# Attention output in row-tiled products, and its projection in the same two PSUM banks

## The chip, the cores and the metric

The kernel runs on one core of a Trainium2 chip. The metric is the time of the whole program on the device, in microseconds (us). Engines: PE multiplies matrices into PSUM (eight banks of 512 f32 columns on 128 partitions), DVE, ACT and POOL do the other arithmetic, SP issues most DMAs. Each engine runs its own instructions in order, and semaphores tie them.

## The reference, cut to what matters

128 samples of 64 tokens with 128 features. A layer normalisation and a cross-attention with 16 heads of 8 features stand first, then three feed-forward blocks of two linear layers each (weights dequantised, with low-rank parts), whose middle has a layer normalisation and a GELU.

```python
q = heads(layernorm(x) @ Wq.T + bq); k = heads(ctx @ Wk.T + bk); v = heads(ctx @ Wv.T + bv)
score = einsum('bhij,bhkj->bhik', k, q) / sqrt(8)
attn  = softmax(score, axis=1)                       # over the heads
out   = einsum('bhik,bhij->bhjk', attn, v)           # sum over the keys i
x     = x + (out as tokens x 128) @ Wo.T + bo
x     = x + ffn(layernorm(x))                        # three blocks
```

The softmax runs over the heads, not over the keys.

## The kernel before

The tokens are cut into 16 chunks of 512 (four tiles of 128 tokens, eight samples). A chunk has four pairs of samples. On its 128 partitions a pair has the keys of its two samples, 64 each; for every head there are 64 queries. Every engine walks the chunks c = 0 to 17 in four steps p = 0 to 3 (`chunk(c, par, half)`); chunks 2 to 11 are a hardware loop over two chunks, the rest is written out. Step n = 4c + p works on several pairs at once:

- PE: the scores of pair n + 1 into `score_ps` (L1439); the shift of pair n by its maxima (L1591, behind DVE); something for chunk c + 2 (context transposes, query, key or value projection); a part of the output projection of an earlier chunk (`project_out`, L1427); probabilities times values of pair n - 2 into `att_ps` (L1648, behind POOL and, for a chunk's first pair, behind ACT); remainders or input transposes for chunk c + 2.
- DVE: maxima over the heads for pair n (L840); in step 1 the input statistics of chunk c + 3 (L624); for pair n - 1 the sum over the heads (L856) and its reciprocal (L859); in step 3 the residual addition for chunk c - 2, out of `wo_ps` (L863).
- ACT: the exponentials of pair n (L1164), and most evacuations, among them `att_ps` to `att_t` in step 2 (L1203) and the value blocks (L1083) in step 3.
- POOL: probabilities times the reciprocal for pair n - 1 (L527), and the small variance work of inputs and layers.

**Probabilities times values.** The values lie in `v_diag`: for each pair and head a block of 32 columns. The rows are the pair's 128 keys. Of the 32 columns a head fills 8 for sample 0 and 8 for sample 1 (on the other sample's rows these are zero), and the other 16 belong to its neighbour head. A product takes 128 rows, 32 columns of weights and 64 queries; four go to four column places of the array (`tile_position=(0, 32 * grp)`), and 16 products do a pair. The result holds eight heads by two samples on 128 partitions, once for each half `o` of the heads: the columns of `att_ps` are 256 for each half.

**Output projection.** Since a sample's features lie in two column halves, mixed with the other sample's, the weight `wo_t` exists four times (`[P, 2, 2, P]`: half, sample), with zeros in between. A tile of tokens takes two f32 products into `wo_ps`, behind a row product of 512 columns that opens the bank and puts the bias there. `bias_rows` and `project_out(0)` stand in step 3, tiles 1, 2 and 3 in the steps 0 to 2 of the next chunk, and the third raises `s_wo`. The bank may be opened when DVE has added the chunk before (`s_x2`).

**The turn.** Some feed-forward steps for the first chunks are put among the last chunks by a table (`EARLY`), and a third and a fourth one are written out by hand. `third_step_closes` on PE, at the end of (15, 3), is a second layer (L1694) behind ACT's first GELU; `third_step` on DVE stands in (16, 0) and takes in its result (L898). After chunk 17 the feed-forward steps run in a loop of their own.

Lines of the change: L660 and L712 to L720 (DVE: weight copies), L863 (addition), L1005 to L1017 (ACT: seeds, layers), L1083 (value blocks), L1151, L1203, L1353 to L1362 (PE: weight transposes), L1391, L1423, L1611 to L1654.

## Time and profile before

| | us |
|---|---|
| median of three runs | 358.87 (358.61 to 361.41) |
| the profiled execution, whole | 358.84 |
| its span, first to last instruction | 356.9 |
| PE busy | 340.4 |
| DVE busy | 327.8 |
| ACT busy | 289.0 |
| POOL busy | 267.3 |

The span is what the profiler sees of the program; about 2 us of the time lie around it. A row of the timeline gives the start, the length from the first start to the last end, engine, line, what is written from what, and how many records were merged. An f32 product that isn't a transpose has two records, each with a load of weights beside it (PEld). Records of one engine overlap at their ends, so what one thing costs is read from start to start.

### The profile page before, as it was taken

The numbers are of one execution on the slowest core, as the hardware profiler recorded it, in microseconds if no ns is written. First come the engines' busy times: TensorE is split into PE (matmuls) and PEld (weight loads), VectorE is DVE, ScalarE is ACT, GpSimd is POOL, SyncE is SP. The second block draws the span as 40 slices with busy tenths as digits, with TensorE's granted clock in tenths as the row PEclk, the third lists the DMA queues.
The fourth block names the chain that finished last, engine by engine and source line by source line (L and its number), as shares of the span: only waits on it lengthen the run. The fifth ranks groups of instructions, "written<-read, shape, count | busy, mean of one in ns | idle before, by whom it ended". The sixth has DMA issues, their size and how long they took to land.

```text
span 356.9 us, 13104 instructions
## 1 busy us (share of the span) xinstructions
PE 340.4 (95%) x4808; PEld 254.6 (71%) x4808; DVE 327.8 (92%) x822; ACT 289.0 (81%) x588; POOL 267.3 (75%) x288
## 2 busy tenths in 40 slices
PE   7979999999999999999999989978999999999995
PEld 6546567667767766766766767856888888888874
DVE  7889999999999999999999999878999999988774
ACT  4688888888878878887887868488989999999982
POOL 6448888877987987897799998878777778774231
PEclk9999999999999999999999999999999999999999
DMA  7978557648646744854753400000110001110112
GB/s 204 239 243 266 172 163 217 209 129 245 195 132 202 222 157 150 264 167 140 222 162 109 151 2 2 2 1 3 30 32 29 29 29 41 50 32 29 42 48 89
DMA packets 54530, 43.29 MB, mean 121 GB/s; under 512 B 4624, under 2 KB 48608, under 8 KB 54496
## 3 DMA queue, kind: packets, MB, share of 16 engines
q1 hardware_dynamic: 53920, 42.31, 39.4%
q10 hardware_dynamic: 576, 0.53, 0.5%
q8 instruction: 21, 0.34, 0.4%
q14 instruction: 13, 0.11, 0.1%
HBM read 26.05 MB, written 16.78 MB: 120 GB/s over the span
## 4 chain that ended last, share of the span: by engine, by line
PE 61%; DVE 23%; issue 6%; ACT 5%; POOL 4%; DMA 1%; DVEq 0%; ACTq 0%; POOLq 0%
PE score_ps L1687 8%; DVE zsum L856 6%; PE att_ps L1648 6%; PE score_ps L1591 6%; DVE negmax L840 5%; PE wo_ps L1427 5%; PE score_ps L1439 4%; PE score_ps L1781 3%; PE work L1463 3%; PE work L1774 3%; DVE st L886 3%; PE att_ps L1781 2%; PE work L1476 2%; PE work L1469 2%; PE score_ps L1681 2%
## 5 line engine op out<-in xcount | busy, mean ns | idle before, releaser
L527 POOL TENSOR_TENSOR probs<-probs,rz 128x1024 f32<-128x1024 f32 x64 | 136.3, 2141 | 27.3 <-DVE rz L859 27.3
L578 POOL TENSOR_TENSOR rs<-ve,minus_half 128x4 f32<-128x4 f32 (+1 forms) x47 | 55.7, 1186 | 34.7 <-DVE ve L786 24.1
L856 DVE TENSOR_REDUCE zsum<-probs 128x64 f32<-128x1024 f32 x64 | 77.3, 1208 | 2.4 <-ACT probs L1164 2.3
L1164 ACT ACTIVATE probs<-score_ps 128x1024 f32<-128x1024 f32 x64 | 65.6, 1025 | 14.5 <-PE score_ps L1591 13.9
L840 DVE TENSOR_REDUCE negmax<-score_ps 128x64 bf16<-128x1024 f32 x64 | 75.2, 1176 | 0.8 <-PE score_ps L1439 0.8
L1427 PEld LDWEIGHTS wo_ps<-wo_t,att_t 128*128 128x128 f32 x256 | 36.9, 191 | 13.4 <-issue 12.0
L1687 PEld LDWEIGHTS score_ps<-lin_t,h 128*128 128x128 f32 x304 | 36.9, 191 | 11.3 <-DVE h L939 7.1
L1648 PE MATMUL att_ps<-probs,v_diag 128*32 128x64 f32 x2048 | 43.4, 224 | 1.1 <-POOL probs L527 0.7
L1252 ACT ACTIVATE z<-score_ps,rs 128x128 f32<-128x128 f32 x152 | 43.6, 383 | 0.6 <-POOL rs L578 0.6
L1687 PE MATMUL score_ps<-lin_t,h 128*128 128x128 f32 x304 | 39.7, 278 | 1.9 <-DVE h L939 1.9
L1648 PEld LDWEIGHTS att_ps<-probs,v_diag 128*32 128x32 f32 x2048 | 32.8, 109 | 10.9 <-POOL probs L527 2.7
L1591 PE MATMUL score_ps<-negmax,ident_bf 128*128 128x512 bf16 x128 | 38.7, 384 | 0.6 <-DVE negmax L840 0.5
L1427 PE MATMUL wo_ps<-wo_t,att_t 128*128 128x128 f32 x256 | 38.1, 275 | 0.0
L859 DVE RECIPROCAL rz<-zsum 128x64 f32<-128x64 f32 x64 | 35.4, 553 | 2.2
L886 DVE BATCH_NORM_STATS2 st<-score_ps 128x6 f32<-128x128 f32 x152 | 33.7, 284 | 3.5 <-PE score_ps L1687 2.5
L1439 PE MATMUL score_ps<-q_stack,k_stack 64*64 64x128 f16 x1024 | 26.5, 222 | 1.9 <-DMA k_stack<-k_parts 0.8
L1439 PEld LDWEIGHTS score_ps<-q_stack,k_stack 64*64 64x64 f16 x1024 | 16.6, 106 | 13.4 <-issue 11.0
L476 POOL TENSOR_TENSOR half_rstd<-veps,minus_half 128x4 f32<-128x4 f32 x16 | 16.5, 1029 | 5.7 <-DVE veps L636 2.4
L1031 ACT ACTIVATE xln<-x_all,half_rstd 128x128 f32 (+1 forms) x60 | 19.0, 391 | 0.9 <-POOL half_rstd L476 0.9
L1263 ACT ACTIVATE g<-score_ps,cols 128x512 f32<-128x512 f32 x21 | 16.8, 800 | 2.8 <-PE score_ps L1681 2.8
L1774 PEld LDWEIGHTS work<-lin_t,g 128*128 128x128 f32 x104 | 13.7, 192 | 6.2 <-issue 6.2
L1083 ACT ACTIVATE v_diag<-work 64x512 f32<-64x512 f32 x30 | 17.6, 586 | 0.3
(278 smaller groups left out, 692.7 us busy)
## 6 DMA issues: line engine op xcount, KB each, us to landing
q_parts<-parts SPq DMA_DIRECT2D x15, 512.0 KB, 3.5
k_stack<-k_parts SPq DMA_DIRECT2D x30, 256.0 KB, 3.3
q_stack<-q_parts SPq DMA_DIRECT2D x60, 128.0 KB, 2.9
x_all<-in_x SPq DMA_DIRECT2D x16, 256.0 KB, 3.9
ctx_sb<-in_ctx SPq DMA_DIRECT2D x16, 256.0 KB, 3.7
k_parts<-parts SPq DMA_DIRECT2D x16, 256.0 KB, 2.9
out<-x_all SPq DMA_DIRECT2D x15, 256.0 KB, 2.3
q_parts<-parts SPq DMA_DIRECT2D x4, 128.0 KB, 2.3
```

Of the source, the lines that this page charges most:

```text
L527: nc.gpsimd.tensor_tensor(e[:, :, :, :], e[:, :, :, :], by_query.broadcast_to([P, BANDS, SEQ, ADJ]), ALU.mult).then_inc(s_probs, 1)
L578: nc.gpsimd.tensor_tensor(rs2[v][:, lo:hi], ve2[v][:, lo:hi], minus_half[:, lo:hi], ALU.pow).then_inc(p_rs[v], 1)
L840: nc.vector.tensor_reduce(negmax[p % 2][:, :], score_ps[p % 2][:, :].rearrange("p (h k) -> p k h", k=SEQ), AX_X, ALU.max, negate=True).the ...
L856: nc.vector.tensor_reduce(zsum[q][:, :], probs[(p - 1) % 4][:, :, :, :].rearrange("p u k s -> p k u s"), AX_XY, ALU.add).then_inc(s_zsum, 1)
L886: ins = nc.vector.bn_stats(st2[v][:, lo + i, :], src[:, TILE * i:TILE * (i + 1)])
L1164: nc.scalar.activation(probs[p][:, :, :, :], score_ps[p % 2][:, :].rearrange("p (u s k) -> p u k s", s=ADJ, k=SEQ), ACT.Exp, scale=SCALE). ...
L1252: ins = nc.scalar.activation(z[v][0][:, t, :], src[:, TILE * t:TILE * (t + 1)], ACT.Copy, scale=rs2[v][:, lo + t:lo + t + 1])
L1427: ins = nc.tensor.matmul(wo_ps[:, TILE * t:TILE * (t + 1)], att[:, o, TILE * u:TILE * (u + 1)], wo_t[:, o, b, :], start=False, stop=o == 1 ...
L1439: ins = nc.tensor.matmul(score_ps[mp % 2][SEQ * b:SEQ * (b + 1), c0:c0 + 2 * SEQ], k_stack[mb][half_rows, grp, k0:k0 + SEQ], q_stack[mb][h ...
L1591: ins = nc.tensor.matmul(score_ps[p % 2][:, CHUNK * o:CHUNK * (o + 1)], ident_bf[:, :], negmax[p % 2][:, :].unsqueeze(1).broadcast_to([P, ...
L1648: ins = nc.tensor.matmul(att_ps[32 * grp:32 * (grp + 1), c0:c0 + SEQ], v_diag[mb][:, v0:v0 + 32], probs[mp][:, band(hd), :, hd % ADJ], sta ...
L1687: ins = nc.tensor.matmul(dst[:, TILE * t:TILE * (t + 1)], hk[:, TILE * t:TILE * (t + 1)], lin_t[:, 2 * v - 2, :], start=v == 1 and t == 0, ...
```

## The change

- `v_diag` keeps its 32 columns for each head, but a head's 8 columns now hold the same columns for both samples: four heads share a place, each on its own 8 of the 32 columns. A product takes the 64 rows of one sample (`tile_position=(SEQ * b, 32 * grp)`), so that the samples are apart in the result: sample b of every pair goes to bank b of a two-bank tensor `pair_ps`, columns 0 to 255. A pair has 32 products instead of 16. The value blocks are one ACT instruction on 128 rows instead of two on 64.
- All 16 heads by 8 features now lie on the 128 partitions, so the projection takes one f32 product a tile with one weight `wo_t` `[P, P]`. It writes columns 256 to 511 of the same two banks. Since the bank is opened by the attention's first product, each tile has a row product of 128 columns for its bias.
- On PE, tile 0 is projected in step 2, tiles 1 and 2 in step 3, tile 3 in step 0 of the next chunk, which raises `s_wo`. On DVE the addition stands in step 1. The chunk's fourth attention product waits for the addition of the chunk before (`s_x2`).
- `ident`-based weight work shrinks: no memset of `wo_split`, one copy, one transpose, a narrower evacuation. A turned layer (4) goes from (0, 2) to (0, 1) on PE, the seeds on ACT from (1, 0) to (0, 3), and the attention's first and third products in chunk 0 wait for these.
- For c = 16 the addition of chunk 14 stands in step 0, ahead of `third_step`.

```diff
-        att_ps = ps("att_ps", [P, CHUNK])
-        wo_ps = ps("wo_ps", [P, CHUNK])
+        pair_ps = ps("pair_ps", [P, 2 * CHUNK])
+        att_ps, wo_ps = pair_ps[:, 0:CHUNK], pair_ps[:, CHUNK:]
...
+        def attention_columns(b, mp):
+            c0 = CHUNK * b + SEQ * mp
+            return slice(c0, c0 + SEQ)
+        def projected_tile(t):
+            c0 = CHUNK * (t % 2) + 2 * TILE + TILE * (t // 2)
+            return pair_ps[:, c0:c0 + TILE]
...
-                nc.vector.memset(wo_split[:, :, :, :], 0.0).then_inc(s_zero, 1)
...
+            def add_attention(k):
+                dve.wait_ge(s_wo, k + 1)
+                added = pair_ps[:, :].rearrange("p (b w u d) -> p w u b d", b=2, w=2, u=2)[:, 1]
+                x_k = x_all[:, k, :, :].rearrange("p (u b) d -> p u b d", b=2)
+                nc.vector.tensor_tensor(x_k, added, x_k, ALU.add).then_inc(s_x2, 1)
...
+                    if p == 1 and live(c - 2) and not (isinstance(c, int) and c == NCHUNK):
+                        add_attention(c - 2)
...
-                    if p == 3 and live(c - 2):
-
-                        dve.wait_ge(s_wo, c - 1)
-                        nc.vector.tensor_tensor(x_all[:, c - 2, :, :],
-                                                wo_ps[:, :].rearrange("p (t d) -> p t d", t=TPC),
-                                                x_all[:, c - 2, :, :], ALU.add).then_inc(s_x2, 1)
...
                     if isinstance(c, int) and (c, p) == (NCHUNK, 0):
+                        add_attention(c - 2)
                         third_step()
...
-                for b in range(2):
-                    dst = v_diag[par][SEQ * b:SEQ * (b + 1), :].rearrange("p (u a e) -> p u a e", a=4, e=16)
-                    ins = nc.scalar.activation(
-                        dst[:, :, 0:4:3, DH * b:DH * (b + 1)],
-                        src[SEQ * b:SEQ * (b + 1), :].rearrange("p (u s j) -> p u s j", s=2, j=DH), ACT.Copy)
-                ins.then_inc(s_v, 1)
+                dst = v_diag[par][:, :].rearrange("p (u a j) -> p u a j", a=16, j=DH)[:, :, 0:16:5, :]
+                nc.scalar.activation(dst, src[:, :].rearrange("p (u s j) -> p u s j", s=SLOTS, j=DH),
+                                     ACT.Copy).then_inc(s_v, 1)
...
-            def project_out(t, att):
+            def project_out(t, att, opens=False):
 
                 b, u = t % 2, t // 2
-                for o in range(2):
-                    ins = nc.tensor.matmul(wo_ps[:, TILE * t:TILE * (t + 1)], att[:, o, TILE * u:TILE * (u + 1)],
-                                           wo_t[:, o, b, :], start=False, stop=o == 1, skip_group_check=True)
-                return ins
+                nc.tensor.matmul(projected_tile(t), pick_row[:, 1, :], bias3[:, :], start=opens, stop=False,
+                                 skip_group_check=True)
+                return nc.tensor.matmul(projected_tile(t), att[:, b, TILE * u:TILE * (u + 1)], wo_t[:, :], start=False,
+                                        stop=True, skip_group_check=True)
...
+                        elif mp == 2 and isinstance(mc, int) and mc == 0:
+                            pe.wait_ge(s_seed, 1)
+                        elif mp == 3 and some(mc):
+                            pe.wait_ge(s_x2, mc)
+                        pe.nop(nofuse=True)
+                        for s in range(SLOTS):
+                            for grp in range(GROUPS):
+                                hd = SLOTS * grp + s
+                                v0 = 32 * (HEADS * mp + hd)
+                                for b in range(2):
+                                    rows_b = slice(SEQ * b, SEQ * (b + 1))
                                     ins = nc.tensor.matmul(
-                                        att_ps[32 * grp:32 * (grp + 1), c0:c0 + SEQ], v_diag[mb][:, v0:v0 + 32],
-                                        probs[mp][:, band(hd), :, hd % ADJ], start=(mp == 0 and o == 0 and s == 0),
-                                        stop=False, skip_group_check=True, tile_position=(0, 32 * grp))
+                                        pair_ps[32 * grp:32 * (grp + 1), attention_columns(b, mp)],
+                                        v_diag[mb][rows_b, v0:v0 + 32], probs[mp][rows_b, band(hd), :, hd % ADJ],
+                                        start=mp == 0 and s == 0, stop=False, skip_group_check=True,
+                                        tile_position=(SEQ * b, 32 * grp))
```

PE in the loop, the last two steps of a chunk (2 and 3), before:

```order
L1469 MATMUL work<-ctx_tr,w_t_k 128x512
L1427 MATMUL wo_ps<-wo_t,att_t 128x128 x2
L1648 MATMUL att_ps<-probs,v_diag 32x64 x16
...
L1476 MATMUL work<-w_t_v,ctx_tr 128x128 x4
L1616 REGISTER_ALU
L1411 MATMUL wo_ps<-bias,pick_row 128x512
L1427 MATMUL wo_ps<-wo_t,att_t 128x128 x2
L1648 MATMUL att_ps<-probs,v_diag 32x64 x16
```

and after (L1643 is the attention product, L1426 and L1428 are the row product and the product of a projected tile):

```order
L1469 MATMUL work<-ctx_tr,w_t_k 128x512
L1643 MATMUL pair_ps<-probs,v_diag 32x64 x32
L1426 MATMUL pair_ps<-bias,pick_row 128x128
L1428 MATMUL pair_ps<-wo_t,att_t 128x128
...
L1476 MATMUL work<-w_t_v,ctx_tr 128x128 x4
L1426 MATMUL pair_ps<-bias,pick_row 128x128
L1428 MATMUL pair_ps<-wo_t,att_t 128x128
L1426 MATMUL pair_ps<-bias,pick_row 128x128
L1428 MATMUL pair_ps<-wo_t,att_t 128x128
L1643 MATMUL pair_ps<-probs,v_diag 32x64 x32
```

The wide row product is gone, a tile has one product, and 32 narrow products stand where 16 were.

DVE at the turn, from the reciprocal of pair 62 to the sum into h of the third step, before:

```order
L859 RECIPROCAL rz<-zsum 128x64
L863 TENSOR_TENSOR x_all<-wo_ps,x_all 128x512
L856 TENSOR_REDUCE zsum<-probs 128x64
L859 RECIPROCAL rz<-zsum 128x64
L881 BN_STATS st_1<-x_all 128x6 x4
L886 BN_STATS st_1<-work 128x6 x4
L898 SCALAR_TENSOR_TENSOR h_0<-score_ps,res_cols,h_0 128x512
```

and after (L787 is the addition, L870 and L873 are the sum and the reciprocal, L907 the sum into h):

```order
L873 RECIPROCAL rz<-zsum 128x64
L870 TENSOR_REDUCE zsum<-probs 128x64
L873 RECIPROCAL rz<-zsum 128x64
L787 TENSOR_TENSOR x_all<-pair_ps,x_all 128x512
L890 BN_STATS st_1<-x_all 128x6 x4
L895 BN_STATS st_1<-work 128x6 x4
L907 SCALAR_TENSOR_TENSOR h_0<-score_ps,res_cols,h_0 128x512
```

The addition seen first before was that of chunk 13; the one seen after is that of chunk 14, which stood behind the third step.

PE at the same place, around the second layer of the third step, before:

```order
L1648 MATMUL att_ps<-probs,v_diag 32x64 x16
L1694 MATMUL score_ps<-g,lin_t 128x512
L1427 MATMUL wo_ps<-wo_t,att_t 128x128 x6
L1648 MATMUL att_ps<-probs,v_diag 32x64 x32
L1687 MATMUL score_ps<-lin_t,h_0 128x128 x8
```

and after (L1697 is the second layer, L1690 the first layers):

```order
L1643 MATMUL pair_ps<-probs,v_diag 32x64 x32
L1697 MATMUL score_ps<-g,lin_t 128x512
L1643 MATMUL pair_ps<-probs,v_diag 32x64 x32
L1426 MATMUL pair_ps<-bias,pick_row 128x128
L1428 MATMUL pair_ps<-wo_t,att_t 128x128
L1643 MATMUL pair_ps<-probs,v_diag 32x64 x32
L1690 MATMUL score_ps<-lin_t,h_0 128x128 x8
```

Chunk 14 has one tile left to project behind the second layer, where it had three.

## Rows read from the trace of the kernel before

**Rows 1.** The page: busy times and the chain that ended last.

```profile
PE 340.4 (95%) x4808; PEld 254.6 (71%) x4808; DVE 327.8 (92%) x822; ACT 289.0 (81%) x588; POOL 267.3 (75%) x288
...
PE 61%; DVE 23%; issue 6%; ACT 5%; POOL 4%; DMA 1%; DVEq 0%; ACTq 0%; POOLq 0%
```

**Rows 2.** Busy time of each engine in two stretches of a chunk each.

```profile
core 0: us, PE busy (x) PEld busy (x) DVE busy (x) ACT busy (x) POOL busy (x), PEclk, DMA share, GB/s
92.00:104.80 12.80, 12.71 (x243) 8.82 (x242) 12.66 (x18) 10.44 (x18) 10.59 (x11) 1.00 0.62 184
104.80:117.40 12.60, 12.60 (x242) 8.82 (x242) 12.29 (x18) 10.37 (x18) 10.23 (x10) 1.00 0.63 187
```

**Rows 3.** Timeline, DVE: start, length, engine, line, what.

```profile
43.67 1.16 DVE L840 TENSOR_REDUCE negmax<-score_ps 128x64 bf16<-128x1024 f32 x1
...
149.38 0.86 DVE L624 BATCH_NORM_STATS2 stats<-x_all 128x6 f32 x4
150.15 1.20 DVE L856 TENSOR_REDUCE zsum<-probs 128x64 f32<-128x1024 f32 x1
...
151.85 1.16 DVE L840 TENSOR_REDUCE negmax<-score_ps 128x64 bf16<-128x1024 f32 x1
152.93 1.20 DVE L856 TENSOR_REDUCE zsum<-probs 128x64 f32<-128x1024 f32 x1
154.17 0.55 DVE L859 RECIPROCAL rz<-zsum 128x64 f32<-128x64 f32 x1
154.64 1.16 DVE L840 TENSOR_REDUCE negmax<-score_ps 128x64 bf16<-128x1024 f32 x1
...
157.70 0.63 DVE L863 TENSOR_TENSOR x_all<-wo_ps,x_all 128x512 f32 x1
158.25 1.21 DVE L840 TENSOR_REDUCE negmax<-score_ps 128x64 bf16<-128x1024 f32 x1
```

**Rows 4.** Timeline, PE, in chunk 10.

```profile
149.27 0.69 PE L1648 MATMUL att_ps<-probs,v_diag 128*32 128x64 f32 x32
149.89 0.66 PE L1457 MATMUL work<-ident,xln 128*128 128x128 f32 x4
150.48 0.42 PE L1439 MATMUL score_ps<-q_stack,k_stack 64*64 64x128 f16 x16
150.83 0.61 PE L1591 MATMUL score_ps<-negmax,ident_bf 128*128 128x512 bf16 x2
151.31 1.12 PE L1463 MATMUL work<-xln_t,w_t_q 128*128 128x512 f32 x2
152.28 0.61 PE L1427 MATMUL wo_ps<-wo_t,att_t 128*128 128x128 f32 x4
```

**Rows 5.** Groups by line and shape: in all, mean ns of one, idle before.

```profile
L1083 ACT ACTIVATE v_diag<-work 64x512 f32<-64x512 f32 x30 | 17.6, 586 | 0.3
...
L660 DVE MEMSET wo_split<- 128x512 f32 x1 | 0.5, 485 | 0.1
```

**Rows 6.** Timeline at the turn: POOL, PE, DVE, with idle time before and its releaser.

```profile
214.93 2.14 POOL L527 TENSOR_TENSOR probs<-probs,rz 128x1024 f32<-128x1024 f32 x1 [0.57 <-DVE rz L859]
...
224.20 1.12 PE L1694 MATMUL score_ps<-g,lin_t 128*128 128x512 f32 x2 [0.43 <-ACT g L1263]
...
225.36 0.75 DVE L898 SCALAR_TENSOR_TENSOR h<-score_ps,res_cols,h 128x512 f32<-128x512 f32 x1 [0.23 <-PE score_ps L1694]
...
226.96 1.64 POOL L578 TENSOR_TENSOR rs<-ve,minus_half 128x8 f32<-128x8 f32 x1 [1.02 <-DVE ve L811]
...
230.02 1.04 POOL L605 TENSOR_TENSOR z<-z,nmr 128x512 f32<-128x512 f32 x1
...
229.78 1.95 PE L1427 MATMUL wo_ps<-wo_t,att_t 128*128 128x128 f32 x16
231.56 0.60 PE L1681 MATMUL score_ps<-ident,z 128*128 128x128 f32 x4
...
233.03 1.12 PE L1694 MATMUL work<-g,lin_t 128*128 128x512 f32 x2 [0.43 <-ACT g L1263]
```

77 lines of the change are left out of this document (29 added, 48 removed).

## The prediction

> **What bounds the kernel now.** I read four views, in this order. First the page's busy times: PE is busy 95% of the span and DVE 92%, and the chain that ended last is PE for 61% and DVE for 23% [rows 1]. Two engines are nearly full, so a gain on one stops where the other begins. Second the stretches of one attention chunk each: PE is busy for 12.60 of 12.60 us and 12.71 of 12.80 us, DVE for 12.29 and 12.66 us, ACT and POOL for 10.2 to 10.6 us, at the full granted clock (1.00, the 2.4 GHz level) [rows 2]. The reader should see that no engine but PE and DVE can set the pace here.
>
> Third, DVE's order within a chunk [rows 3]. Taken start to start, a pair without extras costs 1.08 us from the maxima to the sums (151.85 to 152.93), 1.24 us to the reciprocal and 0.47 us to the next maxima: 2.79 us. A chunk has four pairs, the statistics of a later input (149.38 to 150.15: 0.77 us) and the residual addition (157.70 to 158.25: 0.55 us). So DVE needs 4 x 2.79 + 0.77 + 0.55 = 12.48 us. The maxima of chunk 2 start at 43.67 and those of chunk 11 at 158.25 [rows 3], which is 114.58 us for nine chunks, 12.73 us each. So DVE loses 0.25 us a chunk. The place is the sums behind the maxima, which wait for exponentials whose shift PE issues late. That is all that a faster PE can give back in the loop.
>
> Fourth, the turn from attention to the feed-forward steps, 214 to 235 us [rows 6]. It is a chain over POOL, ACT, PE and DVE, and there the order of single instructions matters.
>
> **PE in the loop.** Before, the output projection of a chunk is one bf16 row product of 512 columns (about 0.22 us; the shift is two of that size, 150.83 to 151.31 with a short wait) and 16 records (eight f32 products of two records) of 0.11 us each, as in the 16 records from 229.78 to 231.56, 1.78 us [rows 4, 6]. After, each of the four tiles has one f32 product and one 128-column bf16 row product. For the latter I take a quarter of the 0.22 us, 0.06 us. PE sheds 8 x 0.11 = 0.89 us and nothing on the row products (0.22 against 4 x 0.06). The turns of the array into and out of the narrow tiles stay at one per pair.
>
> **The unknown: 64 records instead of 32 for a pair's probabilities times values.** Now 32 records (16 products with 128 rows, 32 columns, 64 moving columns) take 0.62 us from their start to the next group's (149.27 to 149.89) [rows 4]. With 64-row tiles a pair has 32 products, 64 records, on eight places of the array instead of four, so each place still runs four products one behind the other. If the places set the time it stays 0.62 us. If the stream of records sets it, the 32 further records cost what the present ones do without the hand-over to the next group. The hand-over I read from the scores, whose 16 records take 0.35 us to the next start (150.48 to 150.83): two such groups would hold 32 records and two hand-overs in 0.70 us, the attention group holds 32 and one in 0.62, so a hand-over is about 0.08 us [rows 4]. That leaves 0.54 us more, 1.16 us a group. Ends: 0 and +0.54 us a pair. I take 0, because the scores are the nearest row: they already run 64-row tiles, two row halves into two banks, and 16 of their 128-column f16 records take no longer than 0.35 us, half of the 32 f32 records; but both rows have about the same time per record (0.35/16 = 0.022 and 0.62/32 = 0.019 us), so they don't exclude that the stream is the limit.
>
> The Trainium skill ("TensorEngine Tiling (Array Packing)", Tiling Modes) counts eight independent 64 by 32 tiles, and under Gotcha 1 asks that different row tiles write different PSUM banks, which a bank per sample does. By that rule the group stays at 0.62 us; no row here shows eight tiles at once. The Trainium skill ("TensorE: Matmul & The Clock Gate", Back-to-back issue gap) gives a floor of about 25 ns per matmul however small N is. By that 64 records would take 1.6 us. The trace disagrees for four tiles: 0.019 us each [rows 4].
>
> With 0, PE needs 12.6 - 0.9 = 11.7 us a chunk, 0.75 us less than DVE's 12.48. DVE then sets the pace: nine chunks give 9 x 0.25 = 2.3 us; for the others I count nothing. **Term 1: -2.3 us.**
>
> Is a step still covered? The addition moves from the fourth pair to the second, behind the statistics, where DVE's step becomes 2.79 + 0.77 + 0.55 = 4.11 us and the other three 2.79 us. PE's last product of the previous chunk's attention now waits for that addition. Queued behind it on PE are the query remainder, the next scores and the next shift. Counted from the start of the maxima: the addition is done after 1.08 + 0.77 + 0.63 = 2.48 us; PE reaches the waiting product after maxima 1.16, shift 0.48 and query projection 0.97 (151.31 to 152.28) [rows 4], 2.61 us. So the wait costs nothing, with 0.1 us to spare. The addition in turn waits for the last projected tile, which PE issues one step earlier, behind 0.62 us of attention and 0.3 us of projection. POOL's product for a pair (2.14 us [rows 6]) still lands a step ahead.
>
> **The start.** DVE loses a memset of 0.485 us ahead of the first statistics [rows 5] and three of four weight copies, PE three of four transposes, ACT 384 of a copy's 512 columns. The later ones lie beside DMA waits. The memset is on the chain to the first scores, but only part of that chain is DVE's: -0.3 us (0 to -0.5). ACT writes the value blocks with one instruction of 128 rows instead of two of 64 at 586 ns [rows 5]; ACT is not the bound in the loop, and in chunk 0 the seed copy takes the freed place: -0.1 us. **Term 2: -0.4 us.**
>
> **The turn.** Two places cost. (a) In chunk 15 the addition of chunk 13 now stands ahead of the sums of pair 60, so its reciprocal comes 0.55 us later, and POOL's product at 214.93 waited for exactly that for 0.57 us. From it the chain runs through POOL's variance and scale, ACT's normalisation, the exponential of pair 63, the table load and the GELU to PE's second layer at 224.20 [rows 6]. **Term 3: +0.5 us.** (b) In chunk 16 DVE adds chunk 14 ahead of the third feed-forward step, before behind it. It needs the last projected tile of chunk 14, which PE issues behind that second layer: 224.20 + 0.97 (two 512-column f32 records, as the query projection) + 0.1 hand-over + 0.62 attention + 0.06 + 0.22 projection + 0.2 until its end is seen (the group at 229.78 is that much longer than the way to the next start) = 226.4. DVE, idle until then, adds for 0.55 us, takes two sets of statistics of 0.77 us and reaches the sum into h at 228.5 instead of 225.36, 3.1 us late. POOL's scale started 1.6 us behind that sum and its last product into z ended at 230.02 + 1.04, 4.1 us later [rows 6]: now at 230.1 and 234.2. PE transposes that z (0.44 us, as four records of 0.11) and starts the next second layer at 234.7 instead of 233.03. **Term 4: +1.7 us.** PE's own saving there (18 records of 0.11 us, 2.0 us, less four small row products net of the wide one) is hidden behind these waits. After the turn nothing changes.
>
> **Sum.** -2.3 - 0.4 + 0.5 + 1.7 = -0.5 us. The profiled execution took 358.84 us around a span of 356.9 us, practically the median of 358.87 us: 358.84 - 0.5 = 358.3 us. A measurement of this kernel tells about 1% (3.6 us) from no change. Own range of this case: 355.5 to 361 us.
>
> **Rivals.** *R1, the stream of records binds, slower.* A pair costs 0.5 us more on PE. The place is the group of L1648, and it decides from the point where PE's chunk passes DVE's: 0.75 us a chunk, 0.19 us a pair, so from 0.81 us a group. At +0.5 us PE needs 11.7 + 2.0 = 13.7 us a chunk against 12.73 now: +1.0 us for about 12 chunks, 12 us, and no gain from term 1; terms 2 to 4 add 1.8 less about 1 that overlaps: some 370 to 372 us. Half that price gives 362 to 363 us. For it: equal time per record in scores and attention. Against it: scores already run on four places at row and column positions. The Trainium skill's floor per matmul ("TensorE: Matmul & The Clock Gate", Back-to-back issue gap) would be a harder form of this rival; of the 0.20 I give it 0.01, since four tiles already run under it.
> *R2, the turn costs nothing, faster.* If the late third step is absorbed (the chain at 231.56 is PE's now, and PE's work there shrinks by 1.9 us), terms 3 and 4 fall and part of PE's saving shows: 358.84 - 2.7 - 1.6 = 354.5 us. For it: PE's records at 229.78 run straight into the transposes at 231.56 [rows 6]. Against it: DVE's in-order queue.
> *R3, PE and DVE hold each other up in the loop.* The spare 0.1 us at the new wait is gone, and 0.3 us a chunk are lost on top of no gain: 358.8 + 13 x 0.3 + 1.8 = 364.5 us. Against it: PE waits there with 0.75 us a chunk in hand.
>
> **Chances.** Forecast 0.58, R1 0.20, R2 0.16, R3 0.06. Faster by over 1% (under 355.3 us): R2 mostly, 0.16 with a little of the forecast's edge less what R2 misses. Slower by over 1% (over 362.4 us): R1 and R3 less their mild ends, 0.23. Within 1%: 0.61. The range reaches down to R2 and up into R1: 354.2 to 367 us, which leaves out R1's full price (0.13) and a little below.
>
> **What would show it.** Right: the attention group of 64 records still about 0.6 us from start to next start; PE's busy share in the loop falls to 94% or so and DVE's rises, with maxima of chunks 12.5 us apart; at the turn DVE shows a wait of nearly 3 us before the residual addition of chunk 14. Wrong: attention groups over 0.8 us; maxima 13 us or more apart; a wait of DVE's addition for PE in every chunk; or no wait at the turn.

## The result: 3.4% slower, and the profile after

The changed kernel takes 372.35 us (median of 4 runs, 370.0 to 375.71) against 359.37 us of the kernel before beside it. The ratio is 1.034 (95%: 1.029 to 1.039); it is formed without the execution of 375.71 us, which lies more than 1.5% above the fastest one. I had forecast 358.3 us with a range up to 367, so the forecast is wrong. The profiled execution is that longest one (span 373.6 us), 3.4 us over the median. A second trace of the same kernel, of an execution of 371.93 us, stands beside it wherever the difference matters.

The page of the changed kernel, busy times, chain and two groups, answers to [rows 1]:

```profile
PE 343.9 (92%) x6773; PEld 250.4 (67%) x6773; DVE 329.0 (88%) x818; ACT 278.9 (75%) x572; POOL 266.5 (71%) x288
...
PE 65%; POOL 11%; DVE 8%; issue 6%; ACT 6%; DMA 2%; SPq 0%; ACTq 0%; POOLq 0%; DVEq 0%
...
L1643 PE MATMUL pair_ps<-probs,v_diag 64*32 64x64 f32 x4096 | 57.2, 226 | 8.3 <-issue 5.5
...
L787 DVE TENSOR_TENSOR x_all<-pair_ps,x_all 128x512 f32 (+1 forms) x16 | 11.1, 691 | 12.0 <-PE pair_ps L1428 11.7
```

PE has 3.5 us more busy time than before, though each chunk lost eight products. Its share of the span fell all the same, so PE stands still more often. "issue 5.5" behind the attention group (L1643, L1648 before) is idle time for which the profile names no other engine; that is new. DVE's residual addition (L787) waits 11.7 us for PE.

Busy times of the engines in two loop chunks answer to [rows 2] (us, busy time and instructions of each engine, granted clock of PE, DMA share, GB/s):

```profile
core 0: us, PE busy (x) PEld busy (x) DVE busy (x) ACT busy (x) POOL busy (x), PEclk, DMA share, GB/s
102.40:115.50 13.10, 12.72 (x365) 8.41 (x364) 12.64 (x18) 9.78 (x17) 10.38 (x11) 1.00 0.59 177
115.50:128.30 12.80, 12.75 (x366) 8.55 (x365) 12.52 (x18) 9.85 (x17) 10.41 (x11) 1.00 0.62 187
```

PE is as full as before, and the stretches are 0.2 to 0.3 us longer. PE's timeline in the first of them (start, length, instruction, idle time before) answers to [rows 4]:

```profile
103.68 0.86 PE L1643 MATMUL pair_ps<-probs,v_diag 64*32 64x64 f32 x64
104.85 0.42 PE L1439 MATMUL score_ps<-q_stack,k_stack 64*64 64x128 f16 x16 [0.31 <-issue]
...
111.78 1.02 PE L1469 MATMUL work<-ctx_tr,w_t_k 128*128 128x512 f32 x2
112.73 0.86 PE L1643 MATMUL pair_ps<-probs,v_diag 64*32 64x64 f32 x64
113.53 0.23 PE L1426 MATMUL pair_ps<-bias,pick_row 128*128 128x128 bf16 x1
113.59 0.44 PE L1428 MATMUL pair_ps<-wo_t,att_t 128*128 128x128 f32 x2
```

A group of 64 records takes 0.80 us from start to next start (112.73 to 113.53) where 32 took 0.62 [rows 4]. The median over all groups is 0.80. Looked at record by record, the first 32 start mostly 7 ns apart, in rounds of eight, and reach 0.27 us: the eight places do work side by side. Then a gap of about 0.06 us follows, and from the 33rd on the records come at 12 ns each: the second 32 take 0.38 us.

In the loop that is not the whole loss. Most of it lies in code that is executed once or for the first time. From the starts of the maxima, in us, with the second trace of the changed kernel in the last column:

| stretch | before | after | more | after, second trace |
|---|---|---|---|---|
| start of chunk 0's maxima | 20.11 | 20.70 | +0.6 | 19.74 |
| chunk 0 | 11.05 | 11.05 | 0 | 11.05 |
| chunks 1 to 4 | 50.98 | 57.94 | +7.0 | 54.45 |
| chunks 5 to 11 | 88.69 | 90.25 | +1.6 | 90.24 |
| chunks 12 to 14 | 38.32 | 42.11 | +3.8 | 42.12 |
| chunk 15 to the end | 147.81 | 151.52 | +3.7 | 152.19 |

PE's timeline at two of the places where it stood still, chunks 3 to 4 and 13:

```profile
62.14 0.33 PE L1643 MATMUL pair_ps<-probs,v_diag 64*32 64x64 f32 x13
63.88 0.75 PE L1643 MATMUL pair_ps<-probs,v_diag 64*32 64x64 f32 x51 [1.41 <-issue]
...
72.58 0.38 PE L1411 MATMUL work<-bias_h,pick_row 128*128 128x512 bf16 x1
75.10 1.05 PE L1476 MATMUL work<-w_t_v,ctx_tr 128*128 128x128 f32 x8 [2.13 <-issue]
...
196.96 0.66 PE L1643 MATMUL pair_ps<-probs,v_diag 64*32 64x64 f32 x41
198.69 0.43 PE L1643 MATMUL pair_ps<-probs,v_diag 64*32 64x64 f32 x23 [1.07 <-issue]
```

In the middle of a group, with nothing that the program has it wait for, PE has no instruction. The page's part on DMA queues counts the transfers that bring instructions (packets, MB, share of the engines). In the page of before:

```profile
q8 instruction: 21, 0.34, 0.4%
```

and in the page of after:

```profile
q8 instruction: 29, 0.48, 0.5%
```

Each packet is 16 KB and takes 0.9 to 1.5 us. Outside the repeated passes, up to about 240 us, one starts every 3.3 to 8 us, 5.1 us in the mean, where the mean was 7.0 us before. From about 77 to 185 us, the repeated passes of the loop, there are none. Each of the three stalls stands beside a packet: the first and the third begin 0.1 and 0.3 us behind the landing of one, the second 0.1 us behind the start of one. The three end 1.3 to 1.5 us behind the landing of the packet beside them. So theory **T1**: the doubled number of instructions costs twice, by the pace of the group and by their late arrival. Its rival **T2**: the tiles of 64 rows on two banks cost it.

### The profile page after: what moved, and what is told of

The parts are those of the page before. It is cut to its first block, busy times and chain, and to the rows that moved or that the text cites. A ratio compares the mean times of both kernels' runs of the same rounds, so it can differ in the third digit from the quotient of the medians.

```text
span 373.6 us, 17066 instructions
## 1 busy us (share of the span) xinstructions
PE 343.9 (92%) x6773; PEld 250.4 (67%) x6773; DVE 329.0 (88%) x818; ACT 278.9 (75%) x572; POOL 266.5 (71%) x288
## 4 chain that ended last, share of the span: by engine, by line
PE 65%; POOL 11%; DVE 8%; issue 6%; ACT 6%; DMA 2%; SPq 0%; ACTq 0%; POOLq 0%; DVEq 0%
PE pair_ps L1643 9%; PE score_ps L1690 8%; PE score_ps L1591 7%; POOL probs L537 6%; PE score_ps L1439 5%; PE pair_ps L1428 4%; PE work L1469 3%; PE score_ps L1784 3%; PE work L1476 3%; PE work L1777 3%; PE pair_ps L1784 3%; PE score_ps L1684 2%; DVE st L895 2%; PE pair_ps L1684 2%; ACT probs L1169 2%
## 5 line engine op out<-in xcount | busy, mean ns | idle before, releaser
L870 DVE TENSOR_REDUCE zsum<-probs 128x64 f32<-128x1024 f32 x64 | 77.2, 1206 | 2.0 <-ACT probs L1169 2.0
L1643 PEld LDWEIGHTS pair_ps<-probs,v_diag 64*32 64x32 f32 x4096 | 45.9, 105 | 37.6 <-issue 35.8
L1643 PE MATMUL pair_ps<-probs,v_diag 64*32 64x64 f32 x4096 | 57.2, 226 | 8.3 <-issue 5.5
L1690 PEld LDWEIGHTS score_ps<-lin_t,h 128*128 128x128 f32 x304 | 36.9, 191 | 12.8 <-DVE h L948 6.9
L1690 PE MATMUL score_ps<-lin_t,h 128*128 128x128 f32 x304 | 39.7, 278 | 3.5 <-ACT score_ps L1303 1.4
L873 DVE RECIPROCAL rz<-zsum 128x64 f32<-128x64 f32 x64 | 35.4, 553 | 2.2
L1428 PE MATMUL pair_ps<-wo_t,att_t 128*128 128x128 f32 x128 | 26.8, 306 | 0.3 <-issue 0.3
L787 DVE TENSOR_TENSOR x_all<-pair_ps,x_all 128x512 f32 (+1 forms) x16 | 11.1, 691 | 12.0 <-PE pair_ps L1428 11.7
L1268 ACT ACTIVATE g<-pair_ps,cols 128x512 f32<-128x512 f32 x22 | 17.3, 784 | 5.7 <-PE pair_ps L1684 5.7
L1428 PEld LDWEIGHTS pair_ps<-wo_t,att_t 128*128 128x128 f32 x128 | 19.9, 196 | 0.4
L1476 PEld LDWEIGHTS work<-w_t_v,ctx_tr 128*128 128x128 f32 x120 | 15.8, 191 | 4.5 <-issue 2.3
```

The lines of the kernel that those rows point to most:

```text
L870: nc.vector.tensor_reduce(zsum[q][:, :], probs[(p - 1) % 4][:, :, :, :].rearrange("p u k s -> p k u s"), AX_XY, ALU.add).then_inc(s_zsum, 1)
L1428: return nc.tensor.matmul(projected_tile(t), att[:, b, TILE * u:TILE * (u + 1)], wo_t[:, :], start=False, stop=True, skip_group_check=True)
L1643: ins = nc.tensor.matmul(pair_ps[32 * grp:32 * (grp + 1), attention_columns(b, mp)], v_diag[mb][rows_b, v0:v0 + 32], probs[mp][rows_b, ban ...
L1690: ins = nc.tensor.matmul(dst[:, TILE * t:TILE * (t + 1)], hk[:, TILE * t:TILE * (t + 1)], lin_t[:, 2 * v - 2, :], start=v == 1 and t == 0, ...
```

## The experiments

**The number of records alone.** In the kernel before, each narrow product is cut in two.

```
-    att_ps[.., c0:c0 + SEQ], v_diag[mb][:, v0:v0 + 32], probs[mp][:, band(hd), :, hd % ADJ],
+    for q0 in range(0, SEQ, SEQ // 2):
+        att_ps[.., c0 + q0:c0 + q0 + SEQ // 2], .., probs[mp][:, band(hd), q0:q0 + SEQ // 2, hd % ADJ],
```

> The kernel before, with each narrow product of probabilities times values cut into two of 32 queries: 64 records a pair instead of 32, all in tiles of 128 rows and in one bank, same columns in sum. Theory T1 (the number of records is what costs: beyond about 32 records a group is paced by the stream of instructions, and more instructions come late in code that is executed once): groups of about 0.80 us from start to next start instead of 0.62, so PE's chunk grows from 12.6 by 4 x 0.18 to 13.3 us and the maxima in the loop stand 13.3 us apart; stalls of PE named 'issue' of 1 to 2 us each appear in chunks 1 to 4 and 12 to 14; 370 to 377 us. Theory T2 (the tiles of 64 rows on two banks are what costs, the number of records is nothing): groups of 0.62 to 0.65 us, no new stalls, 359 to 361 us.

Measured 369.61 us (ratio 1.030, 1.029 to 1.032). The group, in 128-row tiles and one bank, takes 0.79 us; its first 32 records reach 0.30 us and the second 32 take 0.36 us:

```profile
112.55 0.86 PE L1650 MATMUL att_ps<-probs,v_diag 128*32 128x32 f32 x64
113.33 0.36 PE L1439 MATMUL score_ps<-q_stack,k_stack 64*64 64x128 f16 x12
```

Chunks of the loop stand 13.25 and 13.7 us apart. T2 falls: for the pace of a group only the number of records matters, not the tiles. The time lies just under the 370 us that T1 gave as its lower end, because the stalls were expected longer than they are: three of 0.4 to 0.7 us outside the loop's jump back, where 1 to 2 us each were expected. The four runs lie within 0.5 us.

> The same cut in the repeated loop alone (chunks 2 to 11); the chunks ahead of it and behind it keep 32 records a pair. T1: groups of 0.80 us in the loop, ten chunks of 13.3 instead of 12.73 us, +6 us, and 1 to 3 us for late instructions in the first pass alone (chunks 2 and 3), none in chunks 12 to 14: 365 to 369 us. If only the pace and not the supply costs: 365 to 366 us without stalls. T2: 359 to 361 us.

Measured 367.89 us (1.025, 1.024 to 1.027). Chunks 13 and 14 are back at 12.52 us, the value of before; chunks 3 and 4, first passes and the jump back, take 14.35 and 14.21 us with 'issue' stalls up to 0.54 us.

**Half of the records in the changed kernel.** Half of the products of probabilities and values are left out. In `for s in range(SLOTS)` of the group, `SLOTS // 2`: everywhere, only where `c` is a number (code executed once), or only in the loop.

> The changed kernel with only the first two of four products of each place of the array: half of the probabilities times values is left out, 32 records a pair in tiles of 64 rows, as many records as before the change. All else, the moved additions and the projection with one product a tile among it, stays. T1: groups of about 0.45 us or less, PE is no bound in the loop, maxima 12.5 us apart as DVE's floor has it, no 'issue' stalls over 0.35 us; what is left of the change is terms 1 to 4: 357 to 360 us. If the moved work itself (waits between DVE and PE, the order of the additions, the start) made the change slow: 365 us or more.

Measured 362.49 us (1.010, 1.009 to 1.012), 2.5 us over the upper end. Groups take 0.40 us, the loop runs at 12.53 and 12.58 us, chunks 13 and 14 at 12.52. From chunk 1's maxima to chunk 12's it is 2.1 us faster than before, as term 1 has it. All of the loss lies behind the start of chunk 15 (+3.7 us). PE's timeline there:

```profile
224.96 0.47 PE L1643 MATMUL pair_ps<-probs,v_diag 64*32 64x64 f32 x32
...
226.70 0.47 PE L1643 MATMUL pair_ps<-probs,v_diag 64*32 64x64 f32 x32 [0.83 <-DVE x_all L787]
228.88 1.35 PE L1690 MATMUL score_ps<-lin_t,h 128*128 128x128 f32 x7 [1.71 <-DVE h L907]
```

DVE's timeline at the same place:

```profile
225.91 0.69 DVE L787 TENSOR_TENSOR x_all<-pair_ps,x_all 128x512 f32<-128x512 f32 x1 [2.58 <-PE pair_ps L1428]
```

And the engines by slices of 1 us, the columns as above:

```profile
226.00:227.00 1.00, 0.30 (x32) 0.33 (x32) 1.00 (x4) 0.00 (x0) 0.00 (x0) 1.00 0.00 0
227.00:228.00 1.00, 0.17 (x23) 0.00 (x1) 1.00 (x6) 0.00 (x0) 0.00 (x0) 1.00 0.06 16
228.00:229.00 1.00, 0.12 (x1) 0.13 (x2) 1.00 (x5) 0.09 (x1) 0.00 (x0) 1.00 0.00 0
229.00:230.00 1.00, 1.00 (x7) 1.00 (x8) 0.93 (x7) 1.00 (x2) 0.32 (x1) 0.74 0.00 0
230.00:231.00 1.00, 1.00 (x7) 1.00 (x6) 0.84 (x5) 0.09 (x1) 1.00 (x1) 0.50 0.00 0
231.00:232.00 1.00, 1.00 (x7) 0.94 (x6) 0.93 (x5) 0.65 (x3) 0.92 (x3) 0.50 0.00 0
232.00:233.00 1.00, 1.00 (x7) 0.94 (x6) 1.00 (x4) 0.49 (x2) 0.86 (x2) 0.55 0.00 0
```

This is term 4 as the prediction described it, DVE's addition waiting 2.6 us for PE and PE then for DVE. The last column but two, the granted clock, is new to the argument: after three slices in which PE was busy 30, 17 and 12% of the time, it falls from 1.00 to 0.50, the 1.2 GHz level, for 3.4 us.

**The order at the turn.** DVE in chunk 16:

```
-                        add_attention(c - 2)
                         third_step()
+                        add_attention(c - 2)
```

> The changed kernel with DVE's addition of chunk 14 put back behind the third feed-forward step in chunk 16. Term 4 of the prediction (1.7 us for that order): 370.6 us against 372.3. If PE's late end of attention sets the turn and not DVE's order: within 0.5 us of 372.3. If PE's last group, which waits for additions, becomes late by it: slower by up to 1 us.

Measured 372.22 us, but the four runs are 366.02, 371.0, 373.44 and 376.44 us, with mean granted clocks of 1.00, 0.994, 0.991 and 0.981. Their median says nothing of 1.7 us. The traces do. Rows of the second layer that follows the third step (L1697), in the first and the second trace of the changed kernel and in the one with the order put back:

```profile
249.67 1.02 PE L1697 MATMUL work<-g,lin_t 128*128 128x512 f32 x2
...
246.12 1.12 PE L1697 MATMUL work<-g,lin_t 128*128 128x512 f32 x2 [0.43 <-ACT g L1268]
...
240.15 1.13 PE L1697 MATMUL work<-g,lin_t 128*128 128x512 f32 x2 [0.43 <-ACT g L1268]
```

Counted from chunk 15's maxima (222.05, 217.60 and 214.51 us) it starts at 27.62, 28.52 and 25.63 us. The first and the third have no fall of the clock at the turn: the order costs 2.0 us. The second has one, and it costs 0.9 us on top. The same edit where stalls for instructions are gone:

> The kernel with half left out everywhere, and DVE's addition of chunk 14 behind the third feed-forward step again. Here the records cost nothing, so the turn shows by itself. Term 4 (1.7 us for the order of that addition): 360.8 us against 362.5; if the fall of the clock at 228 to 234 us came from the long wait of PE that this order makes, it goes too, and the time is 359 to 360 us. If the order costs nothing: 362.5 us.

Measured 358.57 us (10 runs, 357.43 to 359.66), 3.9 us less than the 362.49, and level with before (ratio 1.000, 0.999 to 1.001). In the traces the second layer behind the third step starts at 232.28 us, and in the kernel without the edit at 235.19 us: 2.9 us for the order and the fall of the clock together, for the profiled execution with the edit has no fall. Of the 3.9 us between the medians 1.0 us is left without an account; the profiled execution of the kernel without the edit (361.08 us) is the shortest of its four. The three of the ten runs with a mean clock of 1.00 have a mean of 357.9 us, the seven at 0.993 to 0.995 one of 358.7: 0.9 us go with the lower clock here too.

> The kernel of the half left out with the addition of chunk 14 behind the third step (358.6 us), and besides that the addition of chunk 13 in chunk 15 behind the sums and the reciprocal of pair 60 instead of ahead of them. In the trace without this, that addition waits 0.79 us for PE's last projected tile and takes 0.55 us, and POOL's product of pair 60 starts at 214.68 us, 1.43 us later than before counted from the maxima of chunk 15. If term 3 is that wait and that duration: product about 1.4 us earlier, time 357.2 us. If POOL is late for another reason (PE's wait of 1.70 us for POOL's product at 209.5): 358.6 us. If the last attention group of chunk 14, which waits for the addition, is made late by it: slower than 358.6.

On DVE, beside the edit above:

```
-                    if p == 1 and live(c - 2) and not (isinstance(c, int) and c == NCHUNK):
+                    if p == 1 and live(c - 2) and not (isinstance(c, int) and c in (NCHUNK - 1, NCHUNK)):
...
                         nc.vector.reciprocal(rz[(p - 1) % 4][:, :], zsum[q][:, :]).then_inc(s_rz, 1)
+                    if isinstance(c, int) and (c, p) == (NCHUNK - 1, 1):
+                        add_attention(c - 2)
```

Measured 357.96 us (10 runs, 356.82 to 359.58): 0.6 us less, which the scatter of both doesn't settle. In the traces POOL's product of pair 60 starts 1.5 us earlier, as expected, and the next second layer 0.7 us earlier.

**Where the records cost.**

> The changed kernel with half of the probabilities times values left out (32 records a pair) in the code that is executed once (chunks 0, 1 and 12 to 15), and all 64 records a pair in the repeated loop (chunks 2 to 11). It splits what the records cost: against the kernel with half left out everywhere (362.5 us) only the loop is longer. Theory T1: +0.35 us a chunk in the loop (12.9 against 12.55 us), 3.5 us in ten chunks, some 'issue' stalls in the first pass (chunks 2 and 3) and at the jump back, none in chunks 12 to 14: 365.5 to 368 us. If the late instructions of the first pass are what starts the fall of the clock: up to 371 us, with a spread between executions of several us. If the loop is not what costs: 363 us.

Measured 367.20 us, 4.7 over the kernel with half everywhere. Chunks 2 to 4 take 4.1 us more in the trace, chunks 5 to 11 2.5 us, chunks 12 to 14 nothing (38.32 against 38.33 us). The 2.5 us are 0.36 us a chunk for the pace of the groups alone; by that rate some 1.1 of the 4.1 us are pace too, an estimate.

> The counterpart: half left out in the loop (chunks 2 to 11), all 64 records a pair in the code that is executed once. T1: loop at 12.55 us a chunk without stalls; chunk 1 longer by up to 0.8 us, chunks 12 to 14 by 2.7 to 3.8 us with 'issue' stalls in their groups, and one stall of 0.8 to 1 us in chunk 16: 366 to 368.5 us. If late instructions don't matter and only the groups' 0.4 us a pair do, where PE binds: 364 us.

Measured 365.61 us, 3.1 over. The loop runs at 12.5 to 12.6 us, chunks 12 to 14 take 42.30 us, 4.0 more, with stalls of 1.34 and 1.06 us. The stall of about 0.9 us in chunk 16 that I had expected for lack of instructions is there, but it is something else. It has the same 0.83 us in all seven traces of kernels with the addition ahead of the third step, and in the halved kernel the profile names what ends it: DVE's addition (226.70, above). The group behind it is the chunk's fourth, which waits for that addition. In the first trace of the changed kernel:

```profile
241.27 0.69 DVE L787 TENSOR_TENSOR x_all<-pair_ps,x_all 128x512 f32<-128x512 f32 x1 [2.98 <-PE pair_ps L1428]
...
242.06 0.86 PE L1643 MATMUL pair_ps<-probs,v_diag 64*32 64x64 f32 x64 [0.83 <-issue]
```

The group starts 0.1 us behind the addition's end in every trace of the changed family. So this stall belongs to term 4, not to the instructions. The two parts and the half kernel make 362.5 + 4.7 + 3.1 = 370.3 us, 2 us short of the first median of the whole (372.35) and 3 us short of the second (373.41); the kernel before beside them was 0.45 us shorter than beside the half kernel.

**The scatter.**

> The changed kernel once more, unaltered, for the spread of its executions. Theory: stalls for late instructions, and the falls of the granted clock that follow them, differ from execution to execution, so times lie between 366 and 376 us and the mean granted clock is lower in the longer ones; the execution profiled has other stall lengths at the same places than the first (2.1 us at 72.6 us, followed by 12.2 of the next 16.5 us in chunk 4 at a clock under full). If the 375.7 us were one disturbed execution: all within 1 us of 372.

Measured 373.41 us (6 runs, 371.41 to 375.08). The run with a mean clock of 0.999 is the shortest, the one with 0.981 the longest. The profiled one (371.93 us) has no stall of the kind of 2.13 us ahead of the jump back and no fall of the clock there; in the first trace of the changed kernel both are. The first trace's slices of 1 us there:

```profile
72.00:73.00 1.00, 0.96 (x19) 0.45 (x8) 0.96 (x2) 0.80 (x2) 1.00 (x2) 1.00 0.92 213
73.00:74.00 1.00, 0.00 (x0) 0.00 (x0) 1.00 (x2) 1.00 (x3) 1.00 (x1) 1.00 1.10 328
74.00:75.00 1.00, 0.00 (x0) 0.00 (x0) 1.00 (x2) 0.97 (x4) 1.00 (x2) 1.00 0.90 314
75.00:76.00 1.00, 0.90 (x9) 0.89 (x9) 0.96 (x2) 0.00 (x0) 1.00 (x1) 1.00 0.11 31
76.00:77.00 1.00, 1.00 (x8) 0.91 (x5) 0.09 (x1) 0.60 (x1) 1.00 (x2) 0.60 0.79 256
77.00:78.00 1.00, 1.00 (x61) 0.80 (x64) 0.00 (x0) 0.00 (x0) 1.00 (x1) 0.50 0.84 246
```

The stall of 2.13 us is followed by the fall. It lasts 3.4 us; the 12.2 us at a clock under full of which the expectation speaks are not in the trace. Chunks 3 and 4 take 14.49 and 16.53 us there, 14.82 and 13.05 us in the second trace. In the second trace the fall stands at 240 us, behind waits of 0.83 and 1.32 us at the turn, while its stall of 1.79 us in chunk 3 is followed by none.

**What decides the stalls.** Nops ahead of PE's first wait, and a nop ahead of each group of the cut kernel.

> The changed kernel with 64 nops at the start of PE's program, ahead of its first wait: the code behind them lies 64 instructions (4 KB of a 16-KB packet) later, nothing else changes. If where a packet's edge falls within a group of 64 records decides the stalls: the same stalls at other places and of other lengths, and a time that differs from 372 us by more than 2 us either way. If the stalls belong to the code's position in time (DMA traffic, the state of the buffers): stalls of 0.8 to 2 us at the same groups as now (61, 193, 208 and 236 us) and 371 to 374 us.

> The same with 128 nops (8 KB, half a packet). The same two cases: over 2 us away from 372 us with stalls elsewhere, or 371 to 374 us with the stalls where they are.

> The kernel before with each narrow product cut in two (369.6 us) and a nop behind the waits and ahead of each group, as the changed kernel has it. If the nop is what lets the queue run empty: 'issue' stalls of 1 us and more in chunks 12 to 14, a scatter of several us, 371 to 374 us. If the nop costs nothing: 369.6 us within 0.5.

The shifted kernels took 374.11 us (371.59 to 375.58) and 375.20 us (373.52 to 376.72). Both traces stall at the same records as the unshifted kernel: behind the 13th of a group in chunk 3, behind the 41st in chunk 13, the 61st in chunk 14, and ahead of the group in chunk 16 that waits for the addition. Only the lengths differ (chunk 13: 1.07, 0.79 and 1.35 us). That looks as if a packet's edge didn't matter, but the nops shifted nothing. First lines of the pages of the changed kernel, of those with 64 and 128 nops, of the cut kernel, and of the cut kernel with a nop a group:

```profile
span 373.6 us, 17066 instructions
...
span 373.5 us, 17066 instructions
...
span 372.2 us, 17066 instructions
...
span 367.7 us, 17200 instructions
...
span 369.9 us, 17264 instructions
```

The 64 nops ahead of the groups are 64 more instructions, those at the start are none, and PE's first product starts at 1.52 us in all three traces of the changed kernel. By all that the traces show, the two shifted kernels are further executions of the changed one, and the question that they were to settle was not put. (In the trace with 64 nops the maxima start at 24.35 us, 3.7 us later than in the first: that is no stall in the attention.)

The sites themselves answer it. I count PE's instructions in the order of a trace, each record and each load of weights as one, waits and register work with them, and the four repeats of the loop taken out. Between chunk 0's maxima and 245 us, ten traces have 41 'issue' stalls of 0.3 us or more that are neither in front of a pass's first scores nor of the group that waits for an addition; one of 0.33 us in the 16-bit kernel before is left aside. All 41 stand at number 193 or 194 of a stretch of 256, in kernels of different code. And 256 instructions are a packet: the kernel before has 6024 instructions, 23.5 stretches of 256, and 21 packets, the changed one 8011, 31.3 stretches, and 29 packets, and every kernel profiled has two packets fewer than whole stretches. So these stalls stand at the edge between packets. Each ends 1.2 to 1.7 us behind the landing of a packet; where PE passed an edge without a stall, the last packet had landed 1.26 us before at the least.

The cut kernel with the nop took 370.66 us (369.79 to 371.79), 1 us more; its two longer runs had a mean clock of 0.995. Its profiled run has one stall of 1.8 us in chunk 1 and none above 0.45 us behind the loop: the nop is not the difference. Why 64-row tiles stall for 1 us in chunks 13 and 14 where 128-row tiles with as many instructions don't, stays open. Both have 29 packets; what differs is when a packet lands before its edge, and no trace shows what makes one start. A difference that may bear on it is that PE hardly waits for another engine in the cut kernel (96% busy against 92%).

**Fewer records with the whole computation.** POOL writes the probabilities and ACT the value blocks in f16, so each product is one record instead of two:

```
+        probs_h = [sb(f"probs_h{i}", [P, BANDS, SEQ, ADJ], F16) for i in range(4)]
...
-                        nc.gpsimd.tensor_tensor(e[:, :, :, :], e[:, :, :, :],
+                        nc.gpsimd.tensor_tensor(probs_h[(p - 1) % 4][:, :, :, :], e[:, :, :, :],
```

> The kernel before, with POOL's product written as f16 into tiles of its own and the value blocks in f16: each narrow product is one record instead of two, 16 records a pair instead of 32, tiles of 128 rows as before; ACT's exponentials and DVE's sums stay f32. Theory T1 (the time of a group follows its records, and PE has them on its path): groups of 0.35 to 0.4 us instead of 0.62, PE's chunk 11.6 us, the loop at DVE's floor of 12.5 us, 2.1 us less for chunks 1 to 11; nothing is lost at the turn since no order changes: 355.5 to 357 us. If POOL's product becomes slower by writing 16 bits: up to 359 us.

Measured 356.04 us (ratio 0.993, 0.991 to 0.995): 0.7% less than the kernel before, and the time is as T1 forecast it. A group takes 0.24 us, less than the 0.35 to 0.4 expected. The loop is at DVE's 12.51 us in every chunk.

> The changed kernel with the same 16-bit products (32 records a pair in 64-row tiles, the whole computation) and the addition of chunk 14 behind the third step. T1: the same as the kernel of the half left out with that order, 358 to 359 us, no 'issue' stalls over 0.45 us outside the first 25 us, groups of 0.40 us: the tiles of 64 rows cost nothing by themselves. T2 (64-row tiles on two banks are slow when all of the work is in them): over 362 us.

Measured 360.04 us (5 runs, 358.84 to 361.37), 1 over the upper end; every run has a mean clock of 0.994 or less. The group of 32 records in 64-row tiles takes 0.25 us (0.40 expected) and the loop 12.51 and 12.6 us. There is no 'issue' stall of over 0.51 us, and none of 0.3 us at a packet's edge. From chunk 15's maxima to the end it takes 149.8 us where the kernel before in 16 bits takes 147.0, so the turn still costs, but the tiles are free of cost in the loop:

```profile
109.18 0.32 PE L1645 MATMUL pair_ps<-probs_h,v_diag 64*32 64x64 f16 x32 [0.37 <-POOL probs_h L538]
109.43 0.23 PE L1427 MATMUL pair_ps<-bias,pick_row 128*128 128x128 bf16 x1
```

> The same, and the addition of chunk 13 behind the sums of pair 60 as well, so that of the change the tiles, the shorter projection and the moved additions of the loop are left, with half of the records. If both orders at the turn and the records are all that made the change slow: 356.5 to 357.5 us, level with the kernel before in 16 bits or ahead of it by PE's shorter projection, which DVE's floor should hide.

Measured 359.25 us (10 runs, 358.17 to 364.04), not the 356.5 to 357.5 expected. The profiled execution has two falls of the clock, at 36 to 40 us and at 227 to 231 us, behind waits of PE; chunk 1, where the first lies, takes 13.00 us against 12.05 in the trace of the kernel above. So 16 bits don't bring the changed kernel level with the kernel before in 16 bits (356.04 us). That PE waits more because its groups are shorter is my reading; no run shows it.

## Why the prediction was wrong, step by step

**The group ("Ends: 0 and +0.54 us a pair. I take 0").** The term was mis-sized: it is +0.18 us from start to next start, for the cut kernel (+0.17) as for the changed one. Both models were wrong. The places set the time only for the first 32 records; the second 32 take 0.38 us on eight places and 0.36 us on four, so there the records set it. The scores, which I took as the nearest row, have 16 records and never reach that point. Why the pace changes at 32 records no run tells.

**"PE needs 12.6 - 0.9 = 11.7 us".** Summed start to start over two loop chunks and halved, the projection's products fell from 2.15 to 1.20 us, 0.95 as forecast. Groups rose from 2.54 to 3.50 us, where 4 x 0.18 would be 0.72; the stall of 0.3 us at the jump back, every second chunk, is in it, and groups that take up to 0.95 us. The transposes and products that stand ahead of a group now (L1451, L1463, L1469) take 0.28 us more. My reading is that the turn into the narrow tiles was counted with the projection's records before, and that moving these moved it. So PE's chunk became 12.92 us instead of 12.68, and PE went on setting the pace. The decision point of R1, 0.81 us a group, was passed by these extras together, not by the group alone.

**Term 1 (-2.3 us)** measured -2.1 us once the records are halved, as a floor of DVE at 12.5 us a chunk. With all records it is +1.6 us in chunks 5 to 11 and more in the passes ahead of them.

**What the prediction had no term for: the supply of instructions.** The stalls of 0.3 us and more at packets' edges make 7.1 of the 16.6 us that the first trace is longer than before, and 4.4 of 12.8 us in the second; the rest is the pace of the groups, the turn and smaller stalls. In the kernel of the changed tiles, all records in code executed once cost 3.1 us, and of the 4.7 us of the loop most lies in its first pass and around its first jump back (4.1 us in chunks 2 to 4 of that trace), pace included. The page of before showed no stall of this kind over 0.29 us; only the count of q8 packets could have led to the question.

**Term 2 (-0.4 us)** can't be told: chunk 0's maxima start at 19.8 to 20.4 us in the five traces with the tiles of before, and at 19.7 to 20.8 us, once at 24.35, in those of the changed family.

**Term 3 (+0.5 us)** came near in time and was too small in its mechanism. In the kernel with halved records POOL's product of pair 60 starts 1.4 us later, not 0.55, counted from chunk 15's maxima, since the addition also waited 0.79 us for PE's last projected tile (1.2 us with all records), which I had counted only for chunk 14. Of the 1.4 us only 0.7 reach the next second layer: the removal gave 0.6 us, within the scatter.

**Term 4 (+1.7 us)** had the right mechanism and nearly the right size: 2.0 us in the traces of the full kernel, where the clock doesn't fall. The fall that can follow the wait, 0.9 us more, I had not priced. The 3.9 us between the medians of the halved kernels hold both and 1.0 us without an account. The wait of PE's last group for the addition (0.83 us) belongs here; the sum had no term for it, and it is covered by PE's wait for the sum into h that follows it.

**Rivals.** R1 named 370 to 372 us, and that was the time. Its place was right and its price wrong (0.54 a pair); at +0.18 us a pair its own sum, 11.7 + 0.7 = 12.4 us, leaves DVE's floor in charge and gives no loss. Its number came out by luck: it holds neither the stalls at packets' edges (4.4 and 7.1 us) nor a fall of the clock, and it charges 1.0 us a chunk where the repeated passes lost 0.2. R2 fell with term 4. R3 (each chunk loses 0.3 us more) is near what the loop did, by another mechanism. Of the signs that I had named, the groups stayed just under 0.81 us and chunks 5 to 11 take 12.8 and 13.1 us in turn, but DVE's addition does wait for PE in every chunk of the loop (0.15 and 0.3 us in turn), and at the turn it waits the nearly 3 us of the forecast (2.98). The Trainium skill ("TensorEngine Tiling (Array Packing)", Tiling Modes) counts eight independent 64 by 32 tiles; the trace agrees for 32 records (mostly 7 ns apart), and it was no guide to a group of 64. By the Trainium skill's floor per matmul ("TensorE: Matmul & The Clock Gate", Back-to-back issue gap) 64 records would take 1.6 us; they took 0.80.

## What to carry to other kernels

Count instructions, not only columns: halving the tile doubles the records, and here a run of tiny products went slower behind its first 32 records (12 ns a record against 8), though the places had the same work. Where code is executed once, count the instruction packets before and after a change, here one for each 256 instructions of PE; each stall at a packet's edge costs its own length and, in some executions, a stretch at half clock behind it. Before reading a test that inserts nops, look in its trace for the nops. An addition that is moved ahead in an in-order queue must be priced with the wait of what it adds, at every place where the code is unrolled.

## What the runs showed that I had not expected

- A group of 64 narrow records takes 0.79 to 0.80 us whether it is in 64-row tiles on two banks or in 128-row tiles on one; 32 f32 records of 64-row tiles take 0.40 us, 32 f16 records 0.25 us.
- Instruction packets of 16 KB hold 256 instructions of PE, 29 packets instead of 21, and stalls of 0.3 to 2.1 us stand at their edges. In the four traces of the changed kernel, the two with nops counted in, their sum is 4.4, 4.8, 6.5 and 7.1 us, and 1.5 us in the shortest run, of the kernel with the order put back (366.02 us). Two sites are in all five: behind the 41st record of a group in chunk 13 and behind the 61st in chunk 14. The cut kernel has 29 packets too and 1.5 us of such stalls.
- Each fall of the granted clock seen in the middle of a trace lasts 3.4 us at the 1.2 GHz level, and came behind one or two idle stretches of PE of 1.7 to 2.5 us in all; other stretches of 1.5 to 1.8 us, such as that of 1.79 us in the second trace, had no fall behind them. The kernels in which PE waits least scatter little (the cut one by 0.5 us, before by 1.2 us in the 17 runs beside the third group of experiments, with one of 361.4 us in the first), the changed one from 370.0 to 375.7 us over ten runs.
